# A row's context split over three steps instead of two, its raw load one step later, its eight maxima in one step

## What is computed

```python
# layer 0, per batch row
q = x @ Wq.T;  k, v = text @ Wk.T, text @ Wv.T;  k_ip, v_ip = ip @ Wk_ip.T, ip @ Wv_ip.T
out = softmax(q k^T * s) v + softmax(q k_ip^T * s) v_ip          # 20 heads, s = 1/sqrt(32)
x = out @ Wo.T + bo + x
...
# layer 1: the same with its own weights; a semantic term per (query, token) is added to the
# image scores, and the image probabilities are scaled by a mask per query
```

## Time and profile before

| | |
|---|---|
| median of 3 runs | 1792.5 us (1791.68 to 1792.95) |
| profiled execution: its time, its span | 1792.31 us, 1790.1 us |
| PE busy | 1759.3 us, 98% |
| DVE busy | 1196.7 us, 67% |
| ACT busy | 778.8 us, 44% |
| POOL busy | 427.4 us, 24% |
| steps of layer 0 | 40, from 148.65 us on |

### The profile page before, as it was taken

One profiled execution on the slowest core, in us unless ns is written; L12 is line 12 of the kernel. 1 busy time (PEld: TensorE's weight loads), 2 busy tenths in 40 slices (PEclk: granted clock), 3 DMA queues, 4 the chain that ended last, 5 costly groups with the idle time before them and its releaser, 6 DMA issues.

```text
span 1790.1 us, 52083 instructions
## 1 busy us (share of the span) xinstructions
PE 1759.3 (98%) x22111; PEld 1422.7 (79%) x22111; DVE 1196.7 (67%) x2905; ACT 778.8 (44%) x1569; POOL 427.4 (24%) x523
## 2 busy tenths in 40 slices
PE   8999999999999999999999999999999999999998
PEld 5668888888888888887567788888888888888885
DVE  5786677767776767554655476767676767676674
ACT  3244454555545454544222243435343435344342
POOL 3032333333342424222100111112121212122120
PEclk9999999999999999999999999999999999999999
DMA  7643444443434343435137152314142324224221
GB/s 285 139 146 126 125 146 126 139 111 131 122 119 129 113 137 111 133 114 187 59 36 190 45 144 68 104 45 136 44 134 54 107 66 122 59 81 106 81 65 47
DMA packets 123871, 198.37 MB, mean 111 GB/s; under 512 B 41736, under 2 KB 110744, under 8 KB 116792
## 3 DMA queue, kind: packets, MB, share of 16 engines
q1 hardware_dynamic: 118456, 168.44, 32.8%
q10 hardware_dynamic: 5184, 26.60, 3.9%
HBM read 133.91 MB, written 60.88 MB: 109 GB/s over the span
## 4 chain that ended last, share of the span: by engine, by line
PE 87%; DVE 7%; ACT 2%; DMA 2%; issue 1%; POOL 0%; ACTq 0%; SPq 0%; DVEq 0%
PE proj L548 60%; PE pv L695 6%; PE proj L516 5%; PE st L672 4%; PE rows L652 4%; PE rows L548 3%; PE rows L653 2%; DVE wparts L1396 1%; DVE arena L1418 1%; ACT arena L1075 1%; DMA cbuf<-wq_dram 1%; DVE w_hl L1418 1%; PE rows L740 1%; DMA k_dram<-arena 0%; DMA arena<-k_dram 0%
## 5 line engine op out<-in xcount | busy, mean ns | idle before, releaser
L548 PE MATMUL proj<-w_hl,cbuf 128*128 128x128 f16 x9600 | 601.1, 219 | 0.0
L548 PE MATMUL proj<-cbuf,w_hl 128*128 128x322 f16 (+1 forms) x3840 | 591.4, 300 | 0.0
L548 PEld LDWEIGHTS proj<-w_hl,cbuf 128*128 128x128 f16 x9600 | 548.5, 98 | 2.0
L548 PEld LDWEIGHTS proj<-cbuf,w_hl 128*128 128x128 f16 x3840 | 367.7, 97 | 163.1
L1308 POOL TENSOR_TENSOR arena<-arena 128x400 f16<-128x400 f32 x240 | 233.3, 972 | 874.4 <-ACT arena L1075 874.4
L1074 ACT ACTIVATE arena<-st,rs 128x400 f16<-128x400 f32 x480 | 288.2, 600 | 271.1 <-DVE st L1712 160.4
L1075 ACT ACTIVATE arena<-st,rs 128x400 f32<-128x400 f32 x480 | 286.9, 598 | 0.0
L1050 ACT ACTIVATE arena<-proj 128x323 f16<-128x323 f32 (+1 forms) x160 | 70.7, 442 | 490.8 <-PE proj L548 490.8
L1631 DVE TENSOR_TENSOR arena<-arena 128x400 f16<-128x400 f32 x240 | 141.5, 590 | 119.4 <-ACT arena L1075 115.7
L695 PEld LDWEIGHTS pv<-arena 128*128 128x128 f16 x3840 | 174.9, 97 | 25.9 <-issue 4.3
L1712 DVE TENSOR_TENSOR st<-st,sem_t 128x400 f32<-128x400 f32 x240 | 135.3, 579 | 87.9 <-PE st L672 86.1
(11 more groups left out here) (171 smaller groups left out, 1646.2 us busy)
## 6 DMA issues: line engine op xcount, KB each, us to landing
arena<-k_dram SPq DMA_DIRECT2D x240, 185.2 KB, 3.6
k_dram<-arena SPq DMA_DIRECT2D x160, 161.2 KB, 2.1
raw<-ctx_dram SPq DMA_DIRECT2D x16, 1290.0 KB, 7.8
c_dram<-cbuf SPq DMA_DIRECT2D x16, 1290.0 KB, 7.3
cbuf<-c_dram SPq DMA_DIRECT2D x14, 1290.0 KB, 8.0
cbuf<-w_dram ACTq DMA_DIRECT2D x24, 640.0 KB, 6.9
arena<-q_dram SPq DMA_DIRECT2D x48, 125.0 KB, 2.6
w_hl<-w_dram ACTq DMA_DIRECT2D x8, 640.0 KB, 10.9
```

Of the source, the lines that this page charges most:

```text
L548: mm = nc.tensor.matmul(out, x[a](k), w[b](k), start=(k == 0 and m == 0), stop=(k == KT - 1 and m == 2))
```

## The change

The split of a row's context takes three steps: ACT takes slices 0, 2, 1 in g = 1, slices 4, 3, 6 in g = 2 and slices 5, 7 in g = 3, behind tile 0, tile 1 and tile 3. On POOL the scaling of 5 and 7 and the low part of 3 move from the end of g = 1 into g = 2, behind its three tiles, and the low parts of 5 and 7 into g = 3. DVE's low parts stay two in g = 1 and two in g = 2. The raw load is issued in g = 3 and g = 4 instead of g = 2 and g = 3, and all eight maxima of every row stand in g = 0, as they did for row 0.

```diff
-SLICES = (0, 2, 1, 3, 4, 6, 5, 7)
+SLICES = (0, 2, 1, 4, 3, 6, 5, 7)
...
-                    if g in (2, 3) and i < B - 2:
-                        load_half(i + 2, g - 2)
+                    if g in (3, 4) and i < B - 2:
+                        load_half(i + 2, g - 3)
...
-                    if g == 2 and i == B - 2:
+                    if g == 3 and i == B - 2:
                         split_done(sp, B - 1)
                         sp.dma_start(wo[0], wo_d[0]).then_inc(wo_in, 16)
-                    if g == 3 and i == B - 2:
+                    if g == 4 and i == B - 2:
...
-                splits = iter(SLICES[4 * (g - 1):4 * g] if l == 0 and i < B - 1 and g in (1, 2) else ())
+                splits = iter(SLICES[3 * (g - 1):3 * g] if l == 0 and i < B - 1 and g in (1, 2, 3) else ())
...
-                if l == 0 and i < B - 1 and g == 1:
-                    chores = iter((lambda: scale_context(r + 1, 3), lambda: None,
-                                   lambda: (split_context(r + 1, 1), split_context(r + 1, 3))))
-                if l == 0 and i < B - 1 and g == 2:
-                    chores = iter((lambda: split_context(r + 1, 5), lambda: split_context(r + 1, 7)))
-                if l == 0 and i < B - 1 and g == 1:
-                    after = (5, 7)
...
+                    behind = {1: {1: (scale_context, 3), 5: (split_context, 1)},
+                              2: {1: (scale_context, 5), 3: (split_context, 3), 5: (scale_context, 7)},
+                              3: {1: (split_context, 5), 3: (split_context, 7)}}.get(g, {})
...
-                    parts = iter(range(4, 8) if i else range(8))
-                if l == 0 and i < B - 2 and g == G - 1:
-                    parts = iter(range(4))
+                    parts = iter(range(8))
```

More of the change, by code:

```diff
@@ L1317, in window @@
                     scale_context(r + 1, 1)
-                chores = iter(())
-                if l == 0 and i < B - 1 and g == 1:
-                    chores = iter((lambda: scale_context(r + 1, 3), lambda: None,
-                                   lambda: (split_context(r + 1, 1), split_context(r + 1, 3))))
-                if l == 0 and i < B - 1 and g == 2:
-                    chores = iter((lambda: split_context(r + 1, 5), lambda: split_context(r + 1, 7)))
-                if l == 0 and i < B - 1 and g == 1:
-                    after = (5, 7)
-                else:
-                    after = ()
+                behind = {}
+                if l == 0 and i < B - 1:
+                    behind = {1: {1: (scale_context, 3), 5: (split_context, 1)},
+                              2: {1: (scale_context, 5), 3: (split_context, 3), 5: (scale_context, 7)},
+                              3: {1: (split_context, 5), 3: (split_context, 7)}}.get(g, {})
                 for j in range(NT):
@@ L1330, in window @@
                         prob_low(u, j)
[L1331 to L1335, removed]
+                        if j in behind:
+                            chore, k = behind[j]
+                            chore(r + 1, k)
                 if exists(u + 1, l) and g == G - 1:
@@ L1728, in context_work @@
                     for _, c in zip(range(count), parts):
-                        context_part(i + 1 + (g == G - 1), c)
+                        context_part(i + 1, c)
                 def low():
```

## The result

The changed kernel takes 1811.8 us at the median (1811.55 to 1813.44, 4 runs), the kernel before 1792.7 beside it: ratio 1.0108, 95% interval 1.009 to 1.0125. It is slower by 19 us. The execution profiled took 1811.55, its span is 1809.4.

A forecast was written before the change was run, and what follows sets the result against it. PE, busy 98% of the span, was taken as the bound, others costing only where it waits. Terms 8.1 - 2.4 + 7.3 + 1.0 + 2.7 + 0.8 = +17.5 on 1792.3 gave 1809.8, median 1810; range 1802 to 1816.

The forecast's parts named there:

- Maxima behind the shift: g = 0 into g = 1, rows 1 to 6: two maxima delay the shift's copy and the context's scale; 6 x 1.35 = +8.1 us.
- End of g = 1: POOL's scaling of slices 5 and 7 leaves the end of g = 1, so PE's turn follows sooner; 0.34 x 7 = -2.4 us.
- Middle of g = 2: DVE and POOL hold each other on SBUF, so DVE's low part 4 ends 1.05 later; 7 rows, +7.3 us.
- The rival in which DVE keeps the ports: Middle of g = 2: DVE goes first, POOL's scaling slips behind it; g = 2 costs 0.7 in all, 1803.4 us; chance 0.18.
- g = 3, +1.0: g = 3 receives two ACT splits and POOL's low parts of 5 and 7; 0.15 x 7 = +1.0 us.
- The load: g = 0: the raw load's second half lands too late in rows 5 and 6, about 1.35 each; +2.7 us.
- The rule that a landing after 11.9 costs what it is later: g = 0: a load landing by 11.9 us into the step costs nothing, later ones cost what they are later.
- 7.8 us later at the median: g = 0: the second half's load lands 7.8 us after issue; the half-row store issued behind it is charged nothing.
- rows 1 to 4 are free: g = 0: SP issues the load some 3.9 us into the step, landing at 11.7, so these rows lose nothing.
- My rival: Load late in every row, from k's slow stores or a transfer shared with the store behind it: +5.7, 1816 us; chance 0.12.
- Before the first step: Row 0's new slice order lets POOL's slice 3 split DVE's two low parts, ending later; +0.8 us (0 to 1.0).

The follow-up runs named there:

- experiment 3: Changed kernel with the raw load issued as early as before and the maxima back in two steps (g = 4 and g = 0): 1798.05 us, ratio 1.0035.
- experiment 4: Kernel before with only all eight maxima of every row put in g = 0, load and split as before: 1800.3 us, ratio 1.0051.
- experiment 6: Changed kernel with the load as early as before and the eight maxima of g = 0 in DVE's gaps, none behind the shift: 1796.6 us, ratio 1.0025.
- experiment 5: Changed kernel with the last two slices' maxima and the maximum over eight moved behind the shift's copy, into g = 1: 1812.55 us, ratio 1.0111.
- experiment 7: Experiment 3 with POOL's scaling of slice 5 in g = 2 moved behind tile 5, slice 3 left behind tile 3: 1794.3 us, ratio 1.0014.
- experiment 8: Experiment 3 with POOL's three g = 2 slices behind tile 5 and row 0's old order: 1790.5 us; then also with experiment 6's maxima: 1788.0 us, ratio 0.9975.
- experiment 1: Changed kernel with the half-row store behind the late load moved from g = 0 to the next row's g = 1: 1812.1 us, ratio 1.0114.

## Why the prediction was right, and where it was not

The forecast was 1810, the median is 1811.8; the sum was +17.5, the profiled spans differ by 19.3.

- **Maxima behind the shift, 6 x 1.35.** Exact, and shown three ways (experiments 3, 4 and 6). The path was right too: DVE's run is late, the scale stands in it, ACT's splits wait for the scale. Experiment 5 narrows it: a copy on time gives nothing back while the scale is late.
- **End of g = 1, -0.34 a row.** Exact: 19.13 against 19.47, and the shift instruction takes 0.18 instead of 0.50.
- **Middle of g = 2, +1.05 a row.** Exact, in its mechanism too: 18.57 against 17.52, L1631 (now L1624) twice at 1.63 and 1.71, and POOL ahead of DVE's low part. The six ends that I worked out for this chain, from the scaling to low part 4, came to within 0.03 once moved by 12.97. The rival in which DVE keeps the ports is out. Experiments 7 and 8 put 0.35 of it on the scaling and 0.7 on slice 3, and take all of it away.
- **g = 3, +1.0.** It is 7 x 0.02 = 0.1. POOL's slice 7 does end about when low part 4 starts, as I placed it, but a little ahead: L1624 takes 0.59, not 0.66, as the timeline there has it.

```profile
666.49 0.59 DVE L1624 TENSOR_TENSOR arena<-arena 128x400 f16<-128x400 f32 x1 [1.89 <-ACT arena L1075]
...
665.25 1.41 POOL L1284 TENSOR_TENSOR cbuf<-raw,cbuf 128x645 f16<-128x645 f32 x1
```

- **The load, +2.7.** This is the term that was mis-sized: 7.3. The rule that a landing after 11.9 costs what it is later held in all six rows. The step that failed is "7.8 us later at the median" for every row, with the store behind it: "I charge it nothing". With the store 0.47 behind, seven of twelve loads (the changed kernel's and experiment 5's) took 8.2 to 9.3; without it all six of experiment 1 took 7.6 to 8.0. In the changed kernel this is 4.4 of the 7.3, by the estimate under experiment 1. The issues were nearly as forecast: 4.25, 5.82 and 5.15 into the step in rows 4 to 6, where I took 3.9, 5.5 and 5.5; with them and 7.8 my 2.7 would have been 2.9. So "rows 1 to 4 are free" failed through the transfers of rows 2 to 4. My rival had this cause in brackets ("its transfer shared with the store behind it"), at a chance of 0.12 and with 8.4 for it.
- **Before the first step, +0.8.** Exact, though the part is 1.8 shorter. Three things add up to that. PE's turn L568 starts at 30.95 instead of 32.32 (-1.37), before any instruction that the change touches. From there to the block of matmuls at the end of this part it is 100.86 instead of 100.04: +0.82. All seven kernels with the new order of slices have 100.85 to 100.88 there, all four with the old one 100.04 to 100.06, so that is the order's price. The block itself takes 15.05 instead of 16.29 (-1.25). Stretches, from 8 to 16 us in the kernel before and the changed one, then the block in both, and in experiment 1:

```profile
8.00:16.00 8.00, 5.45 (x13) 2.76 (x12) 3.06 (x4) 0.51 (x1) 0.00 (x0) 0.79 1.00 419
...
8.00:16.00 8.00, 7.46 (x18) 3.72 (x17) 3.06 (x4) 0.50 (x1) 0.00 (x0) 1.00 1.00 420
...
132.36:148.65 16.29, 16.14 (x176) 12.72 (x177) 6.79 (x24) 1.65 (x4) 2.61 (x5) 0.91 0.62 215
...
131.81:146.86 15.05, 14.67 (x177) 12.18 (x177) 7.02 (x24) 1.88 (x4) 2.05 (x4) 1.00 0.67 232
...
131.83:149.49 17.66, 17.51 (x176) 13.22 (x177) 6.79 (x24) 1.65 (x4) 2.61 (x5) 0.83 0.58 198
```

The granted clock differs: 0.79 against 1.00 in the first stretch (only the kernel before and experiment 5 have 0.79, and both have their L568 at 32.3, all others at 30.8 to 31.1), and 0.91, 1.00 and 0.83 in the block, which PE begins in every kernel after an idle 3.12. Over the eleven kernels the block takes 14.8 to 15.05 at a clock of 1.00, 16.3 to 16.5 at 0.90 or 0.91, and 17.6 to 17.7 at 0.83 or 0.84. In experiment 1 the clock from 131 to 134 us is 0.50, the lower of its two levels (1.2 instead of 2.4 GHz); in the changed kernel it is 1.00 there. Between the layers it is the same: behind an idle 3.8 of PE a stretch takes 20.09 at 0.87 instead of 19.26 at 0.91, which is the 0.8 lost there. Why the clock falls in one execution and not in another is open.

The measured terms are 5.7 (g = 1), 7.4 (g = 2), 7.3 (load), 0.1 (g = 3), -0.3 from short waits of PE in rows 6 and 7 (for k, where the trace names a cause), -1.8 and +0.8 outside the steps: 19.2. The load's +4.6 over my term is partly cancelled by the clock in this pair of profiles (-2.6 ahead of the steps, +0.8 between the layers) and by g = 3 (-0.9). That the total is nearer than its terms is luck.

## What to carry over

Look for a step of the old kernel that already has the new order (here row 0's eight maxima): its length is the best estimate there is, and it was exact to 0.02 us. Ask of an instruction not in which step it stands but what follows it on its engine without a gap, and who waits for that: eight maxima were free in DVE's gaps and cost 1.35 with two of them in the unbroken run that ends with the scale. A transfer that moves to another place meets other transfers there: price it with what is issued right behind it on its queue (here 0.47 us), not only ahead of it. And before a difference outside the changed steps is called unexplained, compare the granted clock of the two stretches.

## What the hardware showed

- **DVE and POOL on SBUF take turns.** From 642.81 to 649.62 of the changed kernel their ends alternate, and none falls within 0.4 of the one before it. The instruction held ends after the release plus its own length less 0.13 to 0.19: DVE's low part 0.43 later (alone 0.56), its slice 0.69 (644.87 - 644.18 and 647.92 - 647.23; alone 0.88), POOL's scaling 1.12 (alone 1.26). The Trainium skill (SBUF — State Buffer, Who interferes with whom) has the lock, and the trace agrees. Who goes first among two that both stand ready is here the one that has waited longer, in every turn of this chain.
- **Two transfers of 1290 KB issued 0.47 us apart** on one queue: the first one took 7.6 to 9.3 instead of 7.6 to 8.0, the second 10.5 to 11.9 where the page of the profile has 7.2 at its median. The spread stays unexplained: in row 5 the load took 7.6 with the store behind it, in row 3 9.2.
- **The granted clock isn't the same in two executions of the same code.** The block of matmuls before the first step, which follows an idle 3.12 of PE, had 1.00 in the changed kernel and 0.83 in experiment 1, and took 15.05 and 17.66.
